# Full-precision products in seven groups a step instead of ten, and the experts chosen behind the second rotation

## Time and profile before

| | |
|---|---|
| median of 3 runs | 2894.42 us (2891.46 to 2895.87) |
| profiled execution | 2893.81 us, its span 2892.0 us |
| busy, share of the span | PE 95%, PEld 85%, DVE 71%, ACT 59%, POOL 70% |
| granted TensorE clock, mean | 0.982 |
| first pass | from the start to about 1.6 ms |

### The profile page before, as it was taken

How to read it: one execution, slowest core, us unless ns; L and a number is a source line. 1 busy time by engine, 2 the same in 40 slices (tenths; PEclk the granted TensorE clock), 3 DMA queues, 4 the chain that set the end, 5 groups by cost and what they waited for, 6 DMA issues and landing times. The chain is left out here.

```text
span 2892.0 us, 65150 instructions
## 1 busy us (share of the span) xinstructions
PE 2744.5 (95%) x21264; PEld 2447.2 (85%) x21264; DVE 2066.9 (71%) x5722; ACT 1700.2 (59%) x4074; POOL 2020.2 (70%) x2070
## 2 busy tenths in 40 slices
PE   2899999999999999999999959999999999999998
PEld 1788888888888888888888848999999999999997
DVE  3577777777777777777777736767676767676766
ACT  1466666666666666666666635656565656555655
POOL 3578888888888888888888724655566656565655
PEclk9899999999999999999999969999999999999999
DMA  6455555444444434444444023233333333424242
GB/s 190 146 179 178 175 169 172 156 124 124 124 123 122 115 113 114 116 124 123 124 124 122 26 57 64 45 66 48 66 47 67 50 66 53 69 43 67 41 70 43
DMA packets 206150, 292.44 MB, mean 101 GB/s; under 512 B 95800, under 2 KB 167819, under 8 KB 206018
## 3 DMA queue, kind: packets, MB, share of 16 engines
q1 hardware_dynamic: 82786, 241.38, 28.5%
q0 software_dynamic: 122880, 47.00, 11.6%
q10 hardware_dynamic: 352, 2.41, 0.3%
HBM read 201.70 MB, written 93.90 MB: 102 GB/s over the span
## 5 line engine op out<-in xcount | busy, mean ns | idle before, releaser
L1505 POOL DMA_INDIRECT out<-arena,who x320 | 595.6, 1861 | 294.1 <-DVE who L1384 180.8
L694 POOL TENSOR_TENSOR arena<-arena 112x896 f32<-112x896 f32 x192 | 402.9, 2099 | 12.8 <-DMA arena<-in_x 12.8
L1478 PE MATMUL bank<-w_dn,hid 128*114 128x192 f32 x3840 | 401.9, 264 | 0.0
L1478 PEld LDWEIGHTS bank<-w_dn,hid 128*114 128x114 f32 x3840 | 390.3, 180 | 0.0
L576 DVE TENSOR_REDUCE top<-bank 114x2 f32<-114x456 f32 (+1 forms) x576 | 349.8, 622 | 46.9 <-PE bank L939 34.7
L1451 ACT ACTIVATE arena<-bank 128x456 f32<-128x456 f32 x320 | 176.4, 551 | 346.0 <-PE bank L1442 335.4
L1296 POOL DMA_INDIRECT moe_rows<-row,slot x256 | 294.0, 1149 | 102.9 <-issue 84.5
L553 ACT ACTIVATE pieces<-bank 64x456 fp32r<-64x456 f32 x384 | 208.1, 542 | 134.0 <-PE bank L915 131.7
L1455 DVE TENSOR_TENSOR arena<-bank,arena 128x456 f32<-128x456 f32 x320 | 201.4, 629 | 96.4 <-ACT arena L1451 83.3
L1438 PE MATMUL bank<-pieces 128*128 128x456 f32 x640 | 241.2, 377 | 20.9 <-DVE arena L1455 13.9
L734 POOL TENSOR_TENSOR qk<-rot_c,qk 114x384 fp32r<-114x384 f32 x256 | 253.2, 1011 | 8.7 <-ACT qk L755 4.3
(11 more groups left out here) (167 smaller groups left out, 6994.9 us busy)
## 6 DMA issues: line engine op xcount, KB each, us to landing
arena<-in_x SPq DMA_DIRECT2D x63, 2352.0 KB, 12.0
arena<-moe_rows SPq DMA_DIRECT2D x82, 363.4 KB
moe_rows<-filler SPq DMA_DIRECT2D x20, 1453.5 KB
out<-h SPq DMA_DIRECT2D x64, 171.0 KB
out<-arena,who POOLq DMA_INDIRECT x320, 5.0
arena<-in_w_t SPq DMA_DIRECT2D x9, 512.0 KB
arena<-in_w_t SPq DMA_DIRECT2D x18, 256.0 KB
moe_rows<-row,slot POOLq DMA_INDIRECT x256, 7.2
```

Source lines behind the costliest of these rows:

```text
L694: nc.gpsimd.tensor_tensor(xin[at.par][:, g, 0:mid], xin[at.par][:, g, 0:mid], xin[at.par][:, g, mid:XF], ALU.add).then_inc(x_folded, 1)
L1478: ins = nc.tensor.matmul(dst, hid2[:, j, h_part, at], w_dn2[e_par][:, j, w_part, :], start=(j == 0 and s % 2 == 0 and part == 0), stop=(j ...
L1505: nc.gpsimd.indirect_dma_start(out=out[:, :], out_offset=bass.IndirectOffsetOnAxis(ap=who[par][:, s:s + 1], axis=0), in_=ys[par][:, s, :], ...
```

## The change

Two lists of a step are put in another order; nothing is added or left out. On TensorE, ring group S3 goes ahead of `turn_xn`, so that `turn_xn`, attention group 0 and the first `make_qk` stand together; C4 and S5 go behind `gate_logits`, so that `turn_xf`, the second `make_qk` and the gate stand together; S7 and C6 go behind `rank`, which then follows attention group 1. On VectorE, maxima 4 and 5 go behind `choose`.

```diff
@@ step_tensor @@
             ring("S0 C0")
             if z:
                 project(pe, z)
-            ring("S1 C1 S2 C2")
+            ring("S1 C1 S2 C2 S3")
             if a:
                 turn_xn(pe, a)
-            ring("S3")
             if t:
                 attend(pe, t, 0)
             if a:
                 make_qk(pe, a, 0)
             ring("C3 S4")
             if z:
                 turn_xf(pe, z)
             if a:
                 make_qk(pe, a, 1)
-            ring("C4 S5")
             if z:
                 gate_logits(pe, z)
-            ring("C5 S6")
+            ring("C4 S5 C5 S6")
             if t:
                 attend(pe, t, 1)
-            ring("S7 C6")
             if z:
                 rank(pe, z)
-            ring("S8 C7 C8")
+            ring("S7 C6 S8 C7 C8")
             if t:
                 attend(pe, t, 2)
@@ step_vector @@
             if a:
                 rotate(dve, a, 1)
-            maxima("4 5")
             if z:
                 choose(dve, z)
-            maxima("6")
+            maxima("4 5 6")
             if p:
                 pool_image(dve, p, 2)
```

## The result

The change makes the kernel slower: 2916.41 us (median of 5 runs, 2909.35 to 2928.4) against 2895.87 (5 runs, 2891.46 to 2902.05), a ratio of 1.0071 with a 95% interval of 1.0053 to 1.009. The forecast was 2905.3 in a range of 2890 to 2914. So the sign was right, and the size, +20.5 us instead of +10.9, was not.

A forecast was written before the change was run, and what follows sets the result against it. Bound by a closed cycle from C6 over VectorE to `turn_shift` and TensorE's order back; +0.21 us in 44 steps and 0.105 in 16 make 10.9 us, so 2905.3 us, range 2890 to 2914.

The forecast's parts named there:

- the one for S3: S3 ahead of `turn_xn`: first `make_qk` waits for ScalarE's copy of turned rows, +0.03 us a step, bounds -0.08 and +0.10.
- `rank` ahead of S7 and C6: TensorE behind attention group 1: C6 comes later by 0.28 + 0.07 - 0.09 = +0.26 us, bounds 0.06 and 0.35.
- The rival with 0.35: Unshared drain ahead of `rank`: term 0.35 instead of 0.26, +0.30 us a step, 2910 us; chance 0.15.
- The gate joined: Gate products behind the second `make_qk`, C4 and S5 behind them: +0.05 us a step, bounds 0 and 0.15.
- the upper bound: Gate term's 0.15: S5 comes about 0.86 us later, so its ScalarE exponential could delay attention group 1.
- `turn_yn`: TensorE comes later and finds VectorE's normalised rows ready: wait of about 0.05 and long first product go, -0.13 us a step.
- where I took half: First sixteen steps: part of the delay falls into ScalarE's waits for landing scatters, so 0.105 us a step instead of 0.21.
- The cycle that I drew: C6 over VectorE to `turn_shift`, 4.33 us, then TensorE's own order to the next C6, about 20.6 us; closed every step.
- the forecast's own sum: Steady step: 0.26 + 0.05 + 0.03 - 0.13 = +0.21 us.
- The faster rival: TensorE's own sum decides, if C6 comes less than 0.1 us later: -0.10 a step, 2888 to 2889 us; chance 0.10.
- "no change": `rank` nearly free behind the attention group, 0.06 us: sum 0.01 a step, 2895 us; chance 0.17.

The follow-up runs named there:

- `choose` alone: Kernel before with the gate products directly behind the second `make_qk` and `choose` ahead of maxima 4 and 5; S3, S7, C6, `rank` unmoved: 2891.74 us, 0.9981.
- C6 first: Changed kernel with S3 back behind `turn_xn`, C6 ahead of `rank` and S7 behind it: 2893.2 us, 0.9989 to the kernel before.

## Why the prediction was wrong, step by step

**The step that failed** is the one for S3: "TensorE's own sum stays as it is, with one boundary less and short products ahead of S3: 0", and then +0.03 with bounds of -0.08 and +0.10 for ScalarE's copy of the turned rows. The runs put +0.29 in its place (after against the kernel with S3 back), of which 0.27 go when S1's exponential is moved and TensorE's order is kept. I followed what reads S3's neighbours and not what S3 itself needs, a free bank. The trace of before had it, on TensorE and ScalarE at the end of C2:

```profile
1016.63 0.52 PE L931 MATMUL bank<-pieces 128*114 128x114 f32 x4
```
```profile
1015.57 0.99 ACT L770 ACTIVATE xn<-h,shifted,rstd 114x192 f32<-114x192 f32 x2 [1.95 <-POOL shifted L719]
1016.47 0.53 ACT L814 ACTIVATE prob<-bank 115x456 f32<-115x456 f32 x1
```

S1's exponential ends at 1017.00, and the next group of TensorE can start at 1016.98. An S3 standing there would start at 1017.04, 0.06 late. The rest comes from the other terms. Counted from L853, the end of that exponential is fixed: at 7.07 and 7.15 us in the loop's two steps (medians), in before and in after alike, as the chain from L853 over the statistics, GpSimd and `norm1_apply` does not pass through `turn_yn`. TensorE starts C2's last product at 7.06 in before and at 6.83 in after, because `turn_yn` and S0 give back 0.21, and could start S3 some 0.09 later, at 6.92. The exponential and the 0.04 from its end to S3 give 7.11 and 7.19: a wait of 0.19 and 0.27, and S3's first product is 0.05 longer behind it (0.46 against 0.41). That is the +0.28. With S3 alone moved, the give-back is missing, and the price is 0.18. By this reckoning it should be under 0.1: in that kernel the exponential ends at 7.17 and 7.27, 0.10 later, because ScalarE's copy of L853's sums (L763) starts at 2.30 behind L853 instead of 2.20. Why it does, no run shows. In the kernel with S3 back the 0.21 stay a gain, which is why undoing S3 brings 0.29: S3's wait was eating what `turn_yn` gave back.

**`rank` ahead of S7 and C6** was right in size and reason: +0.266 against +0.26. S7's first product is still long (0.44 behind `rank`, 0.46 behind the attention group in the earlier trace rows) but not by both amounts at once, and `rank`'s own first product pays no visible price at the attention's edge (0.22 against 0.21). The rival with 0.35 did not come true. There is a gap of 0.35 from the start of the group's last line (L994) to `rank` in after, as there is 0.33 to S7 in before. The Trainium skill (TensorEngine Tiling (Array Packing), section Key Properties) says that a change of tiling mode drains TensorE. The gap does not contradict it, but the rule gives no price, no run separates a drain from the rest of the gap, and the +0.35 of that rival was not what the trace shows.

**The gate joined** was +0.019 instead of +0.05, inside its bounds; the delay of S5's exponential, the upper bound, did not reach attention group 1.

**`turn_yn`** came out at -0.048 for its wait, and its first product's 0.08 went too, as forecast. The reason stands as well: from T0's first product to the end of the normalisation it is 7.06 us in before, after, `choose` alone and C6 first, and 6.15 to 6.21 only where `weigh` was moved, while T0 starts 1.85 ahead of `turn_shift` in after and 1.43 in before. What I missed is another 0.08 at S0. In before, S0 starts 0.40 and 0.57 behind `turn_yn` in the loop's two steps in turn:

```profile
1036.81 0.63 PE L1015 MATMUL bank<-ident,yn 114*97 114x114 f32 x4
1037.38 0.46 PE L964 MATMUL bank<-pieces 128*115 128x456 f32 x1
...
1061.87 0.63 PE L1015 MATMUL bank<-ident,yn 114*97 114x114 f32 x4
1062.27 0.44 PE L964 MATMUL bank<-pieces 128*115 128x456 f32 x1
```

In after it is 0.33 and 0.32. Of the 0.57, some 0.08 are the long first product, and 0.17 come at every second step, that is at the loop's end. Where the rows are ready well ahead of `turn_yn` (0.43 in after, more with `weigh` early), they are gone; with `choose` alone moved the rows are ready 0.17 ahead, and 0.12 at every second step stay. That the loop's end is the place, the trace of before shows by itself, as six steps are written out ahead of the loop: S0 starts 0.57 to 0.62 behind `turn_yn` at all 28 returns of the loop, and 0.40 everywhere else where `turn_yn` waits 0.05 at full clock, also behind the odd step ahead of the loop and where the loop is left:

```profile
1635.56 0.63 PE L1015 MATMUL bank<-ident,yn 114*97 114x114 f32 x4
1635.96 0.44 PE L964 MATMUL bank<-pieces 128*115 128x456 f32 x1
```

Why a wait is needed for it is not shown. That TensorE works through the loop's end while products are still queued, if nothing just ahead of it waits, would fit all of these.

**The sum.** 0.27 + 0.02 + 0.28 - 0.21 = +0.36 by the pieces, +0.35 measured. Over the pass, `rank`'s first sixteen intervals are 3.6 us longer in all (0.22 each, two thirds of the steady value where I took half), the next 43 by 43 x 0.354 = 15.2. That makes 18.8, and the medians differ by 20.5. The profiled execution of after is 12 us above its median (2928.40), and in it the last four intervals are 12.7 us longer than in before, with a granted clock of 0.80 against 0.86 around there. One profile each can't say whether the change has a part in that; the other kernels' last four lie between 83.6 and 98.0 us (before 88.6, after 101.3).

**What held.** The cycle that I drew is the right one. C6 to `turn_shift` is 4.33 in all nine kernels in which S7 stands ahead of C6, whatever else is moved, VectorE idles 1.0 us ahead of maximum 6 and still starts it on time, and `turn_shift` still starts 0.05 behind `make_shift`:

```profile
1013.12 0.63 DVE L576 TENSOR_REDUCE top<-bank 114x2 f32<-114x456 f32 x1 [1.02 <-PE bank L939]
...
1016.89 0.21 DVE L583 TENSOR_TENSOR shift<-top,bank 114x48 f32<-114x48 f32 x1
```

With the S3 term at 0.29 the forecast's own sum would have been 0.47 a step; the missed 0.08 at S0 and 0.03 at the gate bring it to the measured 0.36. The misses had opposite signs, so that the sum is nearer to the truth than the term for S3 is. The faster rival fell at its own test (C6 comes 0.27 later, not under 0.1), and "no change" because `rank` took its full time.

## What to carry to other kernels

When a group of products moves forward in a ring of banks, look up who frees its bank, and follow that chain on the other engine back to something that stays fixed: time given back elsewhere in the cycle makes exactly such a wait longer. Where TensorE is 99% busy in the records, joining kinds of products may be worth nothing, as it was here; the gains lay in two moves that took work off a chain at little cost (`weigh` into VectorE's idle time, C6 ahead of `rank`). And moving work to the end of an engine's step hides it only if nothing at the start of the next step needs that engine soon, and if the loop's return behind it costs nothing: compare the loop's steps one by one, as a mean over both hides it.

## What the runs showed of the hardware

TensorE lost 0.17 us at every second step behind a wait of 0.05 that stood as the last thing ahead of the loop's end, and lost none where the rows came 0.4 us early. It lost it at the loop's returns alone (0.57 to 0.62 from `turn_yn` to S0, against 0.40). VectorE, with `weigh` last in its list, stood idle for 0.52 to 0.59 us at each return, against 0.12 between the loop's two steps.

In the kernel with only `rank` moved, TensorE waited 0.9 to 1.0 us in each step of 26 us, and the granted clock fell for short times (0.96 over 500 to 1500 us, where the others have 1.00). Stretches of 10 us, columns as in the earlier trace rows:

```profile
1040.00:1050.00 10.00, 9.94 (x77) 8.23 (x76) 7.04 (x17) 6.04 (x12) 7.64 (x12) 1.00 0.30 83
1050.00:1060.00 10.00, 9.04 (x84) 7.84 (x83) 6.84 (x24) 4.75 (x11) 9.16 (x12) 0.83 0.11 14
...
1160.00:1170.00 10.00, 8.76 (x90) 7.57 (x90) 7.11 (x25) 6.32 (x15) 9.09 (x12) 1.00 0.36 96
```
```profile
1054.80 0.21 PE L1052 MATMUL bank<-counts,before 114*114 114x8 bf16 x1 [0.96 <-DVE counts L644]
1055.08 0.69 PE L964 MATMUL bank<-pieces 128*115 128x456 f32 x1
```

Behind the wait at 1054.80, S7's first product takes 0.69 instead of the 0.44 at 1162.72: there the granted clock is at the lower of its two levels, 1.2 GHz, and the 0.83 is the mean of a stretch with both. What the engine did before the fall was to wait 0.96 for VectorE. The same wait ahead of `rank` at 1162.44 did not bring the clock down. Affected steps last 26.9 to 31.7 us instead of 26.0. Of the 104.5 us by which this span is longer than before's, 45 are 43 steady steps at 1.05, and 31 more are what the mean step (26.71) has above the undisturbed one (26.0); most of the others lie in the first sixteen intervals (21.2).
